# Two buffers in turn for the squares of both layer norms in a Mamba-2 and ternary feed-forward layer

## What is computed

```python
def _layernorm(x, axis=-1, eps=1e-5):
    m = jnp.mean(x, axis=axis, keepdims=True)
    v = jnp.var(x, axis=axis, keepdims=True)
    return (x - m) / jnp.sqrt(v + eps)

x = L0_attn_u                                   # (8, 2048, 2048), float32
x = x + _L0_attn_ref(_layernorm(x), W_in, ...)  # Mamba-2: projection to 8512, causal conv over 4,
                                                # SSD scan in chunks of 128 (64 heads of 64, state 128),
                                                # gate y * silu(z), RMS norm, projection to 2048
x = x + _L0_ffn_ref(_layernorm(x), w1, w2, w3)  # ternary weights: q = clip(round(w / mean|w|), -1, 1);
                                                # (sigmoid(x q1') * (x q2')) q3', hidden 5632
```

## Time and profile before

| what | value |
|---|---|
| median of three timed runs | 6333.9 us (6260.15, 6333.9, 6707.61) |
| the profiled execution | 6150.35 us |
| its span, slowest core (core 2) | 6148.8 us |
| spans of the eight cores | 6117.1 to 6148.8 us |
| mean granted TensorE clock | 0.800 |
| TensorE matmul busy | 4495.0 us, 73% |
| VectorE busy | 2263.4 us, 37% |
| ScalarE busy | 1476.1 us, 24% |
| GpSimd busy | 573.3 us, 9% |

### The profile page before, as it was taken

The page is one execution under the profiler, slowest core; times in us unless marked ns, Lnnn a source line. Parts: engine busy times, 40 slices in busy tenths (PEclk is TensorE's granted clock), DMA queues, the critical chain, the costliest instruction groups (busy, mean ns, idle before and its releaser), DMA issues.

```text
span 6148.8 us, 59277 instructions; the slowest of 8 cores (6117.1 to 6148.8 us)
## 1 busy us (share of the span) xinstructions
PE 4495.0 (73%) x21030; PEld 2249.6 (37%) x21348; DVE 2263.4 (37%) x2629; ACT 1476.1 (24%) x1787; POOL 573.3 (9%) x1090
## 2 busy tenths in 40 slices
PE   3776777777673676776776388777797764999997
PEld 1333555433221233332332134555543221444443
DVE  1654555411323233333333267555512232111112
ACT  1455333363001323223222112333321001000000
POOL 0001332200000000001000001223300000000000
PEclk9896555599776898988998698555598876999999
DMA  3794000285320535435334142000043220222222
GB/s 108 192 246 152 29 29 29 74 242 131 71 62 21 179 134 183 144 133 197 131 134 173 50 69 49 2 2 2 8 73 72 62 62 31 72 72 79 83 83 89
DMA packets 144886, 577.01 MB, mean 94 GB/s; under 512 B 36947, under 2 KB 39252, under 8 KB 106580
## 3 DMA queue, kind: packets, MB, share of 16 engines
q1 hardware_dynamic: 76468, 398.76, 19.3%
q0 software_dynamic: 68128, 174.44, 12.9%
HBM read 589.57 MB, written 85.98 MB: 110 GB/s over the span
## 4 chain that ended last, share of the span: by engine, by line
PE 61%; DVE 15%; DMA 12%; ACT 7%; issue 4%; POOL 1%; DVEq 0%; ACTq 0%; SPq 0%; POOLq 0%
PE p_ip L1029 11%; PE p_ip L1038 10%; PE p_ip L907 9%; PE p_ip L274 7%; PE p_ip L830 5%; PE p_ip L1085 4%; PE p_w L1085 4%; PE p_ip L723 4%; DMA aX_gslab<-w1T_t 3%; DMA aX_gslab<-w3T_t 2%; DVE aW_woslab L891 2%; DMA aX_gslab<-w2T_t 1%; DVE aW_tscr L375 1%; DVE STATES_bf L377 1%; PE p_ip L284 1%
## 5 line engine op out<-in xcount | busy, mean ns | idle before, releaser
L1029 PE MATMUL p_ip<-aH_h,aW_q 128*128 128x512 bf16 x2761 | 682.3, 406 | 462.0 <-DVE aW_q L1009 404.7
L907 PE MATMUL p_ip<-aA_xy,aW_woslab 128*128 128x512 bf16 x2006 | 522.8, 425 | 251.6 <-DVE aW_woslab L891 248.3
L1038 PE MATMUL p_ip<-aH_h,aW_q 128*128 128x512 bf16 x2760 | 618.9, 379 | 2.9
L1029 PEld LDWEIGHTS p_ip<-aH_h,aW_q 128*128 128x128 bf16 x2816 | 287.6, 103 | 849.8 <-issue 564.8
L274 PE MATMUL p_ip<-aW_stageR,aW_stageL 2*128 2x128 f32 x2048 | 511.2, 427 | 39.3 <-DMA aW_eacsrow<-aW_eacs 39.1
L274 PEld LDWEIGHTS p_ip<-aW_stageR,aW_stageL 2*128 2x128 f32 x2048 | 471.3, 325 | 101.2 <-issue 84.9
L1047 DVE TENSOR_TENSOR aA_hid<-aW_sig,p_ip 128x1024 bf16<-128x1024 f32 x88 | 107.5, 1221 | 1056.5 <-PE p_ip L1038 1045.1
L723 PE MATMUL p_ip<-aH_h,aW_wslab 128*128 128x512 bf16 x1504 | 358.3, 395 | 163.8 <-DMA aW_wslab<-winT_t 72.2
L1044 ACT ACTIVATE aW_sig<-p_ip 128x1024 f32<-128x1024 f32 x88 | 90.1, 1024 | 1536.8 <-PE p_ip L1029 1489.7
L907 PEld LDWEIGHTS p_ip<-aA_xy,aW_woslab 128*128 128x128 bf16 x2048 | 216.9, 107 | 557.5 <-issue 369.0
L1038 PEld LDWEIGHTS p_ip<-aH_h,aW_q 128*128 128x128 bf16 x2816 | 275.6, 98 | 332.1
(11 more groups left out here) (166 smaller groups left out, 6395.0 us busy)
## 6 DMA issues: line engine op xcount, KB each, us to landing
aW_wslab<-winT_t POOLq DMA_DIRECT2D x92, 512.0 KB, 5.3
aX_gslab<-w1T_t SPq DMA_DIRECT2D x44, 1024.0 KB, 8.1
aX_gslab<-w2T_t SPq DMA_DIRECT2D x44, 1024.0 KB, 5.5
aX_gslab<-w3T_t SPq DMA_DIRECT2D x44, 1024.0 KB, 7.0
aW_w1slab<-w1T_t SPq DMA_DIRECT2D x44, 1024.0 KB, 9.6
aW_w2slab<-w2T_t SPq DMA_DIRECT2D x44, 1024.0 KB, 5.9
aW_w2slab<-w3T_t SPq DMA_DIRECT2D x44, 1024.0 KB, 6.0
aW_woslab<-woutT_t POOLq DMA_DIRECT2D x32, 1024.0 KB, 8.3
```

Source lines behind the costliest of these rows:

```text
L907: ev_mm = P.add(T, lambda t, par=par, lh=lh, ec=ec, pb=pb: t.matmul(pb[lh][:, :], B["woslab"][par][:, 128 * ec:128 * ec + 128], B["xy"][:, ...
L1029: ex1 = P.add(T, lambda t, par=par, lh=lh, k=k: t.matmul(B["p_Y"][lh][:, :], B["q1"][par][:, 128 * k:128 * k + 128], B["h1"][:, k, 512 * l ...
L1038: ex2 = P.add(T, lambda t, par=par, lh=lh, k=k: t.matmul(B["p_diff"][lh][:, :], B["q2"][par][:, 128 * k:128 * k + 128], B["h1"][:, k, 512 ...
```

## The change

In both layer norms the squares go to two buffers in turn. The first layer norm takes `sqb@m0` for even slices and a new buffer `sqbX` for odd ones; the second takes `sqb@m5` for even ones and `sqb@m0` for odd ones. The square of slice k waits for the matmuls of slice k-2. The waits that stood on the first square alone (barrier and output DMAs) stand on the first two.

```diff
     B["wslab3"] = arX.alloc("wslab3", [128, 2048], BF16)
+    B["sqbX"] = arX.alloc("sqbX", [128, SEGL], BF16)
...
         ev_smm = ev_umm = None
+        smm_by_k = []
         for k in range(16):
-            evq = P.add(A, lambda a, k=k: a.activation(B["sqb@m0"][:, :], B["u32"][:, k, :], AF.Square),
-                        waits=evu + (wu if k == 0 else []) + [ev_smm])
+            sqbuf = B["sqb@m0"] if k % 2 == 0 else B["sqbX"]
+            evq = P.add(A, lambda a, k=k, sqbuf=sqbuf: a.activation(sqbuf[:, :], B["u32"][:, k, :], AF.Square),
+                        waits=evu + (wu if k < 2 else []) + ([smm_by_k[k - 2]] if k >= 2 else []))
             for lh in range(2):
-                ev_smm = P.add(T, lambda t, k=k, lh=lh: t.matmul(
-                    B["p_diff"][lh][:, :], B["o128b"][:, :], B["sqb@m0"][:, 512 * lh:512 * lh + 512],
+                ev_smm = P.add(T, lambda t, k=k, lh=lh, sqbuf=sqbuf: t.matmul(
+                    B["p_diff"][lh][:, :], B["o128b"][:, :], sqbuf[:, 512 * lh:512 * lh + 512],
                     start=(k == 0), stop=(k == 15)),
                     waits=[evq] + ([pfree[f"p_diff{lh}"]] if k == 0 else []))
+            smm_by_k.append(ev_smm)
...
         ev_rms_mm_guard = [ev_rms_mm] + P.barrier()
         ev_smm = ev_umm = None
+        smm_by_k = []
         for k in range(16):
-            evq = P.add(A, lambda a, k=k: a.activation(B["sqb@m5"][:, :], B["X1"][:, k, :], AF.Square),
-                        waits=[ev_x1k_m4[k], ev_smm] + (ev_rms_mm_guard if k == 0 else []))
+            sqbuf = B["sqb@m5"] if k % 2 == 0 else B["sqb@m0"]
+            evq = P.add(A, lambda a, k=k, sqbuf=sqbuf: a.activation(sqbuf[:, :], B["X1"][:, k, :], AF.Square),
+                        waits=[ev_x1k_m4[k]] + ([smm_by_k[k - 2]] if k >= 2 else [])
+                        + (ev_rms_mm_guard if k < 2 else []))
```

More of the change, by code:

```diff
@@ L927, in build_program @@
         ev_smm = ev_umm = None
+        smm_by_k = []
         for k in range(16):
-            evq = P.add(A, lambda a, k=k: a.activation(B["sqb@m5"][:, :], B["X1"][:, k, :], AF.Square),
-                        waits=[ev_x1k_m4[k], ev_smm] + (ev_rms_mm_guard if k == 0 else []))
+            sqbuf = B["sqb@m5"] if k % 2 == 0 else B["sqb@m0"]
+            evq = P.add(A, lambda a, k=k, sqbuf=sqbuf: a.activation(sqbuf[:, :], B["X1"][:, k, :], AF.Square),
+                        waits=[ev_x1k_m4[k]] + ([smm_by_k[k - 2]] if k >= 2 else [])
+                        + (ev_rms_mm_guard if k < 2 else []))
             for lh in range(2):
-                ev_smm = P.add(T, lambda t, k=k, lh=lh: t.matmul(
-                    B["p_diff"][lh][:, :], B["o128b"][:, :], B["sqb@m5"][:, 512 * lh:512 * lh + 512],
+                ev_smm = P.add(T, lambda t, k=k, lh=lh, sqbuf=sqbuf: t.matmul(
+                    B["p_diff"][lh][:, :], B["o128b"][:, :], sqbuf[:, 512 * lh:512 * lh + 512],
                     start=(k == 0), stop=(k == 15)),
                     waits=[evq] + ([pfree[f"p_diff{lh}"]] if k == 0 else []))
+            smm_by_k.append(ev_smm)
         for k in range(16):
```

## The result

Over 26 runs of each kernel the changed one takes 0.9893 of the time of the one before, 95% interval 0.9857 to 0.9928: 1.1% faster, clear of the measurement's uncertainty, though within 2%. The medians over all runs, 6164.94 us and 6161.87 us before, say nothing of this, since they contain executions in which the cores of one die ran at a lower granted clock; the ratio leaves those out. The lowest times are 6071.8 and 6143.31 us. The profiled execution took 6084.57 us against 6150.35, its span 6083.0 against 6148.8 us. In the new file the squares are at L668 and L935, their matmuls at L671 and L939, the mean's at L678 and L946.

What follows compares the result with a forecast made beforehand. Took the four passes, where ScalarE and TensorE alternate, as serial with the rest (about 151 us of 6149). Four times 17.8 us, 71 us, off the timed median 6333.9 gave 6263 us; range 6069 to 6334.

Steps and rivals of the forecast that it cites:

- Where the kernel is bound, and what the passes can give: Four passes of sums of squares are on the path that sets the end: about 151 us of 6149, the most to win.
- Two buffers: the period: Squares in all four passes: starts 1.15 and 1.21 us apart instead of 2.363, 17.8 us less a pass, 71 us.
- A: Main case: squares overlap matmuls in the four passes, clock stays low; 71 us won, 6263 us, chance 0.62.
- The waits that I put at about 2 us: ScalarE's waits on the squares' matmuls at L665 and L929, 78.7 us together, should shrink to about 2 us.
- The clock stays low in the pass: TensorE stays at the 1.2 GHz level within the four passes, as it did in the scan stage.
- rival B: TensorE's clock rises within the passes: 20.1 us a pass, 81 us won, 6253 us by the median; chance 0.18.
- The row I leaned on: Short matmuls of the scan stage: TensorE busy for 18.14 of 20 us, yet its clock stays 0.50.
- C: The DMA-bound stage behind the first pass swallows that pass's gain: 53 us won, 6281 us; chance 0.05.
- D: Matmul reads and ScalarE writes in the passes hinder each other and still alternate: no gain, 6334 us; chance 0.04.
- E: The high clock is lost in TensorE's dense stretches: 6632 us; chance 0.05.
- 13 of 16: Lowered clock by the Trainium skill's page: estimated 211 us more for the last 968 us alone.
- From the profile to the time: 71 us off the profiled 6150.35 gives 6079 us; off the timed median 6333.9 it gives the forecast, 6263 us.

## Why the prediction was right or wrong, point by point

**Where the kernel is bound, and what the passes can give.** Right. The four passes were serial with all that follows, and nearly all of what they lost in length left the span: 78.3 us at the places, 76 us of the mean span.

**Two buffers: the period.** Right. The squares' starts are 1.15 and 1.21 us apart in turn as long as the clock is low, and where the clock stays low the sixteenth square starts 17.69 us after the first (fewer columns) and 17.66 (2 rows), as the sum had it. In these two kernels the places win 70.1 and 69.1 us of the 226.6: for its own case the 71 us of A were right. The third buffer took the gap away and won nothing. The waits that I put at about 2 us are 3.5.

**The clock stays low in the pass.** Wrong; this step failed. In 25 of 32 passes the clock rose, which is rival B, at 0.18, though later in the pass than B had it; in the other seven it stayed low, as A had it. The rise shortened the passes, 19.8 us with 2 rows, to between 19.05 and 19.32 us on the core shown, and above all the mean's matmuls start at the high level: 7.22 us to the statistics in place of 8.5, and 28.1 in place of 29.6. The places won 78.3 us; A had 71, and B 81 (four times its 20.1 is 80), since B let the clock rise from the start of the pass. The row I leaned on, was busy enough but of another kind: most of its matmuls use one or two rows of the array, and the kernel with 2 rows shows that in the passes this alone holds the clock at 0.50. The sentence of the Trainium skill ("TensorE: Matmul & The Clock Gate", Part 1) on sustained busy work, which I set behind that row, agrees with the 25 passes in which the clock rose. It doesn't tell these from the seven in which it didn't, nor from the 22 with a third buffer, nor from the 32 with 2 rows, in which TensorE was as busy. Why the clock rose in some passes of the same kernel and not in others is open.

**Where the gain could stick (C).** Nowhere but for some 3 to 4 us. The stretch from the first place to the second pass, with the DMA-bound stage of the earlier trace rows in it, is 1759.6 us against 1761.7. The 3 to 4 us more in the feed-forward of the first segment I had not foreseen, and they are not explained.

**The changed kernel doesn't overlap (D).** Did not come, in any of the passes. **The high clock is lost (E).** Did not come: the last stretch has 0.99 as in the earlier trace rows, and from the fourth place to the end it takes 1014.4 us against 1014.1. A clock near the 13 of 16 that the prediction priced there does occur in these runs, though in neither profile of the change: in the profile of the kernel with fewer columns, core 3 has a granted clock of 0.81 from 5800 to 5900 us and a span of 6149.0 us, where core 0 of the same die has 1.00 in the same stretch and 6078.5 us. So one trace without it was too little to call it absent.

```profile
5131.00:6083.00 952.00, 905.11 (x4100) 407.88 (x4182) 186.54 (x236) 44.73 (x44) 0.00 (x0) 0.99 0.24 80
```

**From the profile to the time.** Here two steps failed. The sum gave 6079 us for an execution like the profiled one, and its counterpart took 6084.57; the relative change, 0.9888, is within the interval of 0.9893. That both lie so near is in part luck: core 2, the slowest in both profiles, won some 80 us at its places and not 71, and lost 14 of them to a longer rest (5935.8 us against 5921.8), which is scatter of the size that the two profiles of before show. But I put the forecast at 6263 us, on the median of three timed runs. Of 26 runs of the kernel before, fourteen lie between 6143 and 6165 us, and those three are at 6260 us and above. The profiled execution at 6150 us was the better anchor, and the sum made on it was there in the prediction. 6263 us is more than the kernel before takes in most of its runs; set against their median of 6161.87 us it even has the wrong sign. And I took from the scatter of these three that only 2% could be told from no change, and gave 0.81 to a result within 2%. That is what came, but the comparison has an interval of 0.36% to each side, so a gain of 1.1% is seen, and the forecast should have been called what its sum said: a small gain that shows, with only rivals D and E, 0.09 together, against it.

## What to carry to other kernels

A buffer that two engines hand to and fro costs the sum of their times a round; two buffers cost the time of the slower engine or half the round, whichever is longer (here 1.15 and 1.18 us in place of 2.36), and the gain can be read off the timeline before it is made. First ask, though, what else the waiting engine has to do: here the mean's matmuls, moved into the wait, did more with one buffer (85 us at the places) than the second buffer did by itself (78), and both together won 111 us. And where a few timed runs scatter by 7%, the time of the profile whose rows make the sum is the better anchor of a forecast, and a small gain on the serial path may well be seen when both kernels are run often enough.

## What the runs showed of the hardware

- TensorE's clock rose to the 2.4 GHz level in the middle of 25 of the 32 passes, 6 to 17 us in (28 of 32 in a second profile, 5 to 19 us in), although TensorE's work there was not unbroken: after every second pair of matmuls it waited for 0.20 us. With the same columns and spacing but 2 of the 128 rows in use, it stayed at 1.2 GHz for all of the 19.8 us in all 32 (places 28.7 in place of 26.5 us). With a third buffer it rose in 10 of 32 only. So TensorE's busy share didn't tell in these runs which level it had.
- The clock also fell again in the middle of busy work: in the kernel with one buffer and the mean's matmuls in between it was back at pairs of 1.01 us 26.5 to 28.2 us into all sixteen passes of the second norm, where TensorE waited for 0.92 us a slice, and up again at 30.5 to 31.1 us.
- Two matmuls on different halves of the array's columns ran side by side: four of them took 1.06 us where two full ones take 1.01.
- Two DMAs of 4 MB each issued one behind the other on the same queue landed one after the other, not together: issued at 28.2 and 28.7 us, the halves of u were in at 45.6 and 58.5 us (core 7).
